# One of three norms moved from TensorE to VectorE, and the weight splits one step earlier

## What is computed

```python
def _gemma_mlp(x, gate_w, up_w, down_w):
    g = jnp.einsum('bsh,hi->bsi', x, gate_w)
    u = jnp.einsum('bsh,hi->bsi', x, up_w)
    return jnp.einsum('bsi,ih->bsh', jax.nn.gelu(g, approximate=True) * u, down_w)
rw = jax.nn.softmax(router_logits, axis=-1)
w, sel = jax.lax.top_k(rw, 2); w = w / w.sum(axis=-1, keepdims=True)
dense_w = zeros((B, E)).at[arange(B)[:, None], sel].add(w)
out = sum over e of dense_w[:, e, None, None] * _gemma_mlp(x, skill_gate[e], skill_up[e], skill_down[e])
return x + out + _gemma_mlp(x, shared_gate, shared_up, shared_down)
```

## Time and profile before

| | us |
|---|---|
| median of 3 runs (210.85 to 211.42) | 210.87 |
| the profiled execution: its time | 211.93 |
| the profiled execution: its span, first to last instruction | 210.1 |
| TensorE busy in the span | 205.2 |
| VectorE, ScalarE, GpSimd busy | 123.6, 133.8, 117.9 |

### The profile page before, as it was taken

The page is one execution under the profiler, slowest core; times in us unless marked ns, Lnnn a source line. Parts: engine busy times, 40 slices in busy tenths (PEclk is TensorE's granted clock), DMA queues, the critical chain, the costliest instruction groups (busy, mean ns, idle before and its releaser), DMA issues.

```text
span 210.1 us, 6672 instructions
## 1 busy us (share of the span) xinstructions
PE 205.2 (98%) x2695; PEld 165.0 (79%) x2695; DVE 123.6 (59%) x217; ACT 133.8 (64%) x217; POOL 117.9 (56%) x129
## 2 busy tenths in 40 slices
PE   7999999989999999999999999999999999999995
PEld 2444555445444478899999999999999999999995
DVE  2899657977999988554353444434435435344452
ACT  6283767677989997655656656556565565655650
POOL 3023644359548997665565655655656556565562
PEclk9999999999999999999999999999999999999999
DMA  6999600000000000000010010010010010010011
GB/s 196 391 433 434 296 2 0 0 3 0 2 0 5 0 0 3 0 3 5 3 53 3 0 53 3 3 53 0 3 55 3 3 53 0 3 53 4 3 50 53
DMA packets 2813, 11.70 MB, mean 56 GB/s; under 512 B 352, under 2 KB 608, under 8 KB 2400
## 3 DMA queue, kind: packets, MB, share of 16 engines
q1 hardware_dynamic: 2640, 11.01, 13.1%
q10 hardware_dynamic: 144, 0.26, 0.7%
HBM read 9.18 MB, written 2.10 MB: 54 GB/s over the span
## 4 chain that ended last, share of the span: by engine, by line
PE 93%; DVE 4%; issue 1%; ACT 0%; POOL 0%; POOLq 0%
PE o_ps L664 7%; PE g_ps L646 7%; PE u_ps L646 7%; PE o_ps L663 7%; PE u_ps L645 7%; PE g_ps L645 7%; PE u_ps L644 7%; PE g_ps L644 7%; PE o_ps L662 7%; PE u_ps L612 3%; PE g_ps L612 3%; PE g_ps L614 2%; PE o_ps L627 2%; PE o_ps L625 2%; PE o_ps L626 2%; PE g_ps L613 2%
## 5 line engine op out<-in xcount | busy, mean ns | idle before, releaser
L304 POOL TENSOR_TENSOR h<-h 128x512 f16<-128x512 f32 x92 | 109.2, 1194 | 79.2 <-ACT h L340 57.9
L457 DVE SCALAR_TENSOR_TENSOR h<-gel,sk_factor,u_ps 128x512 f32<-128x512 f32 x64 | 47.8, 747 | 68.0 <-PE u_ps L646 39.0
L335 ACT ACTIVATE gel<-g_ps,sk_gate 128x512 f32<-128x512 f32 x64 | 43.9, 687 | 49.8 <-PE g_ps L646 49.8
L340 ACT CAST h<-h 128x512 f16<-128x512 f32 x92 | 56.0, 609 | 3.5 <-DVE h L457 3.5
L645 PE MATMUL g_ps<-x,wsk 128*128 128x128 f16 x256 | 46.2, 219 | 0.0
L646 PE MATMUL g_ps<-x,wsk 128*128 128x128 f16 x256 | 46.2, 219 | 0.0
L645 PE MATMUL u_ps<-x,wsk 128*128 128x128 f16 x256 | 46.2, 219 | 0.0
L646 PE MATMUL u_ps<-x,wsk 128*128 128x128 f16 x256 | 46.2, 219 | 0.0
L644 PE MATMUL u_ps<-x,wsk 128*128 128x128 f16 x256 | 46.2, 219 | 0.0
L644 PE MATMUL g_ps<-x,wsk 128*128 128x128 f16 x256 | 46.2, 219 | 0.0
L663 PE MATMUL o_ps<-h,wsk 128*128 128x128 f16 x256 | 45.9, 219 | 0.0
(11 more groups left out here) (103 smaller groups left out, 310.1 us busy)
## 6 DMA issues: line engine op xcount, KB each, us to landing
wsk<-skills SPq DMA_DIRECT2D x3, 2048.0 KB, 16.1
outT<-xT SPq DMA_DIRECT2D x7, 256.0 KB, 2.0
xT<-xT SPq DMA_DIRECT2D x2, 768.0 KB, 6.3
wsh<-shared SPq DMA_DIRECT2D x3, 256.0 KB, 3.9
xT<-xT ACTq DMA_DIRECT2D x1, 256.0 KB, 3.5
xT<-xT SPq DMA_DIRECT2D x1, 256.0 KB, 4.6
outT<-xT SPq DMA_DIRECT2D x1, 192.0 KB, 2.6
outT<-xT SPq DMA_DIRECT2D x1, 64.0 KB, 1.5
```

The lines of the kernel that those rows point to most:

```text
L304: nc.gpsimd.tensor_tensor(hidden_lo(t), hidden_full(t), hidden_hi(t), ALU.subtract).then_inc(lo_ok, 1)
L335: nc.scalar.activation(gel[:, t % NG, :], g_ps[t % 2][:, :], ACT.Gelu_apprx_tanh, scale=scale).then_inc(gelu_ok, 1)
L340: nc.scalar.copy(hidden_hi(t), hidden_full(t)).then_inc(hi_ok, 1)
L457: nc.vector.scalar_tensor_tensor(out=h32[:, t % N32, :], in0=gel[:, t % NG, :], scalar=factor, in1=u_ps[t % 2][:, :], op0=ALU.mult, op1=AL ...
```

## The change

The norm of the experts' gate weights no longer comes from `gram`. VectorE takes the largest absolute value per partition over two experts at a time (128x1024) in steps 5, 6, 7 and 8 into a new tile `parts`, then the maximum of the four columns, its square, and `spread_norms` treats it as it does x. The norms of up and down keep their Gram matrices, taken in steps 9 to 12 (before 10 to 13) and 16 to 19 (before 15 to 18). The gate norm's mask is in step 8 (before 9) and its scales in step 10 (before 11); the mask and scales of down come a step later (20 and 22). The pieces of the experts' weights are split at steps 11, 13, ... 33 (before 12, 14, ... 34), the groups 4 to 7 of x at 12, 16, 20 and 24 (before 11, 15, 19, 23), and the experts' tables are made at step 24 (before 23).

```diff
+        parts = sb("parts", [P, E // 2], F32)
+        GRAMS = (K_UP, K_DOWN)
-        TOP_OF = {FIRST: 3 + XF, X_NEXT: 3 + XA, X_REST: 3 + G}
-        K_STEPS = [5, 10, 15]
-        MASK_AT = {3: X_NEXT, 9: K_GATE, 12: X_REST, 14: K_UP, 19: K_DOWN}
-        SPREAD_AT = {4: X_NEXT, 11: K_GATE, 14: X_REST, 16: K_UP, 21: K_DOWN}
+        TOP_OF = {FIRST: 3 + XF, X_NEXT: 3 + XA, X_REST: 4 + G, K_GATE: 4 + XA}
+        PART_AT = {5: (GATE, 0), 6: (GATE, 1), 7: (GATE, 2), 8: (GATE, 3)}
+        K_STEPS = {K_UP: 9, K_DOWN: 16}
+        MASK_AT = {3: X_NEXT, 8: K_GATE, 12: X_REST, 14: K_UP, 20: K_DOWN}
+        SPREAD_AT = {4: X_NEXT, 10: K_GATE, 14: X_REST, 16: K_UP, 22: K_DOWN}
-        SKILL_TABLES_AT = 23
-        X_AT = {3: 0, 5: 2, 8: 3, 11: 4, 15: 5, 19: 6, 23: 7}
+        SKILL_TABLES_AT = 24
+        X_AT = {3: 0, 5: 2, 8: 3, 12: 4, 16: 5, 20: 6, 24: 7}
-        PIECES = {12 + 2 * n: n for n in range(3 * E // EG)}
+        PIECES = {11 + 2 * n: n for n in range(3 * E // EG)}
...
+            def part_top(kind, n):
+                if n == 0:
+                    dve.wait_ge(sk_in[kind], 16)
+                nc.vector.tensor_reduce(parts[:, n:n + 1], wsk32[:, (kind * E + 2 * n) * I:(kind * E + 2 * n + 2) * I],
+                                        AX.X, ALU.max, apply_absolute_value=True).then_inc(part_ok, 1)
             def mask(n):
                 a, b = COLS[n]
-                if n not in K_OF:
+                if n in K_OF and n not in GRAMS:
+                    kind = K_OF.index(n)
+                    dve.wait_ge(part_ok, E // 2)
+                    tops(KC + kind, parts[:, :])
+                if n not in GRAMS:
                     dve.wait_ge(top_ok, TOP_OF[n])
                     nc.vector.tensor_tensor(top2[:, a:b], top[:, a:b], top[:, a:b], ALU.mult).then_inc(diag_ok, 1)
...
                     skill_low(PIECES[t - 1])
                 if t == 0:
                     scales(FIRST)
+                if t in PART_AT:
+                    part_top(*PART_AT[t])
                 if t in TOP_AT:
...
-                        if n == 0 and kind:
-                            pe.wait_ge(diag_ok, K_OF[kind - 1] + 1)
+                        if n == 0 and batch == K_DOWN:
+                            pe.wait_ge(diag_ok, K_UP + 1)
```

More of the change, by code:

```diff
@@ L141, in build @@
         top_ok = sem("top_ok")
+        part_ok = sem("part_ok")
         gram_ok = sem("gram_ok")
@@ L394, in mask @@
                 else:
-                    kind = K_OF.index(n)
-                    dve.wait_ge(gram_ok, kind + 1)
+                    dve.wait_ge(gram_ok, GRAMS.index(n) + 1)
                     nc.vector.scalar_tensor_tensor(out=diag[:, :], in0=n_ps[0][:, 0:P], scalar=NORM_FLOOR,
@@ L403, in scales @@
                 norm = n_ps[1][:, 0:b - a]
-                if n in K_OF:
+                if n in GRAMS:
                     norm = n_all[:, a:b]
                     nc.vector.tensor_reduce(norm, n_ps[1][:, 0:P], AX.X, ALU.max).then_inc(n_red, 1)
-                    dve.wait_ge(n_red, K_OF.index(n) + 1)
+                    dve.wait_ge(n_red, GRAMS.index(n) + 1)
                 nc.vector.tensor_scalar(e_bits[:, a:b], norm.bitcast(U32), 1, EXP_MASK,
@@ L698, in _ @@
                     down_first(1)
-                for kind in range(3):
-                    n = t - K_STEPS[kind]
+                for batch in GRAMS:
+                    kind = K_OF.index(batch)
+                    n = t - K_STEPS[batch]
                     if 0 <= n < 4:
@@ L703, in _ @@
                             pe.wait_ge(sk_in[kind], 16)
-                        if n == 0 and kind:
-                            pe.wait_ge(diag_ok, K_OF[kind - 1] + 1)
+                        if n == 0 and batch == K_DOWN:
+                            pe.wait_ge(diag_ok, K_UP + 1)
                         a = (kind * E + 2 * n) * I
                         for half in range(2):
-                            last = gram(n_ps[0][:, 0:P], wsk32[:, a + half * I:a + (half + 1) * I],
-                                        n == 0 and half == 0)
+                            last = gram(n_ps[0][:, 0:P], wsk32[:, a + half * I:a + (half + 1) * I], n == 0 and half == 0)
                         if n == 3:
```

## The result

The changed kernel takes 212.03 us (median of 8 runs, 211.67 to 212.82) against 211.12 for the kernel before (8 runs, 210.85 to 211.62): ratio 1.0045, 95% interval 1.0028 to 1.0062. It is slower by 0.9 us; no change was forecast, at 210.8, and the slower rival at 211.9 is what happened.

What follows compares the result with a forecast made beforehand. TensorE, busy 205.2 of 210.1 us, was taken as the bound. Four grams leave (1.86), but VectorE's maxima add 4.56 and waits take the gain: 0.1 less, 210.8 us from a 210.87 median; range 209.6 to 212.0.

Steps and rivals of the forecast that it cites:

- the slower rival: Step 14: GpSimd takes the port ahead of the scales, L412 is held 1.14 us; 211.9 us, chance 0.26.
- the maxima hold VectorE's queue for 1.14: Steps 5 to 8: each of four 128x1024 maxima taken as 1.14 us of VectorE, 4.56 against 4.20 idle.
- the down product of step 5: TensorE's product behind GpSimd's subtraction: starts at 25.47 instead of 25.03, after TensorE stands about 1.9 us.
- the square: VectorE's L393, due at 39.24, held by GpSimd's subtraction until 39.94, so the spread comes at 40.0 against 39.60.
- the second piece: Weight split on VectorE in step 14, held behind GpSimd's subtraction until 42.57, then about 1.1, ending at 43.65.
- three of the grams only filled a wait: Steps 5 to 7: of the four removed grams, 1.86 us, only the last, 0.47, would be gained even with shorter maxima.
- Steps 14 to 17: Up norm's mask at 44.33, spread at 44.48 after about 0.5 wait, gate(17) at 45.63 against 46.18: 0.08 ahead overall.
- VectorE falling behind at step 26: Late place where VectorE's dense steps move to; counted within the slower outcome's chance of 0.26, without its own size.
- What spoke against it: Step 14: at 42.63 L412 took only 0.15 beside the start of GpSimd's second subtraction in the kernel before.
- The other rival: The grams' time is kept (faster): about 1.0 less, 209.8 us; keeping all would be 208.0; chance 0.24.
- the down gram's wait: TensorE's 1.00 us before the first down gram at 43.26, saved by moving it a step, half taken back.
- the splits' new steps: Pieces one step earlier, VectorE's dense steps moved to 22 and 26: taken as nothing, 0.5 kept either way.

Runs made afterwards that it cites:

- e3: e4 without the four maxima: the tile of partition maxima is filled with a constant, so the gate norm is not computed; 209.52 us, ratio 0.9911.
- e1: The changed kernel, but in step 14 VectorE does the scales of x's last groups and the up norm's mask ahead of the second weight piece; 211.17 us, ratio 0.9987.
- e2: The changed kernel in its order, but the two scale instructions for x's last groups are written one column at a time; 211.42 us, ratio 1.0003.
- e5: The kernel before, with its Gram matrix for the gate norm, but the splits and experts' tables at the new steps; 215.92 us, ratio 1.0195.
- e4: The changed kernel with the norm by four maxima, but the splits and the experts' tables back at their old steps; 210.4 us, ratio 0.9949.
- e10: e1 with the maximum over x's last group in step 11 instead of 12; 210.89 us, ratio 0.9948 to the kernel before.
- e11: e4 with the maximum over x's last group in step 11 instead of 12; 210.58 us, ratio 0.9934 to the kernel before.
- e9: e4 with the gate maxima in steps 6 to 9, gate mask in 9, its scales in 11, and the maximum over x's last group in 11; 210.36 us, 0.9949.

## Why the prediction was wrong

Its route was right to within 0.14 us from 20.9 to 43.8 us. Forecast and measured: the maxima hold VectorE's queue for 1.14, 1.12 (21.54 to 22.66); `x_low` 23.34, 23.32; GpSimd 24.23, 24.21; the down product of step 5 25.47, 25.43; that of step 8 32.5, 32.56; the square 39.24, 39.38, held for 0.69; the spread 40.0, 40.12; the second piece ends at 43.65, 43.77. The reading that three of the grams only filled a wait is shown by e3.

The step that failed is in "Steps 14 to 17": "The scales of x follow (0.08 before that end, 0.18, 0.1 and the 0.19 of 42.63 to 42.82)". The last term, 0.19, is from the start of L412 to that of the mask, read where nothing held L412. Here it is 1.17 (43.95 to 45.12), because the same instruction, now L425, takes 1.14; the three terms ahead of it came as summed (0.08, 0.18, 0.08). So the mask ends at 45.41 instead of 44.33, the spread goes at 45.47 instead of 44.48, and gate(17) at 46.64 instead of 45.63: 0.08 ahead became 0.92 behind, which is the 0.9 us measured. e1 and e2 show that cause, each by another way round it, and e5 has the hold without the maxima.

The rival had this with its place and its price, at a chance of 0.26 (VectorE falling behind at step 26, counted in it, did not happen: TensorE does not wait there). What spoke against it was misread: in the kernel before, L412 at 42.63 came while L411 still waited for the first subtraction and ahead of the start of the second near 42.69 (41.54 + 1.15); here it came 0.04 after GpSimd's start. e4 has the first order again (42.38 ahead of 42.43, 0.15), e5 the second (43.63 behind 43.59, 1.14). My own numbers put the two at 43.80 and 43.85, in the order that loses, and a duration from a case in which VectorE was first was no evidence for one in which it was second. With that order the rival should have been the forecast. The range, drawn up to that rival's price, ended 0.03 below the measured time. The kernel before took 211.12 beside this result and 210.87 beside the forecast, so that 0.03 says little; what was wrong is the difference of the two kernels, 0.9 us slower where 0.1 faster was summed.

The other rival's reasoning holds in part: the 1.00 of the down gram's wait was there to win, but only once nothing held the mask (e4).

Nothing was taken for the splits' new steps as such, and e10 against e11 shows that this was near enough: their stretches differ by 0.39, and 0.5 was kept for it.

## What to carry to other kernels

Where two engines share a port that one instruction locks whole, the price of a small instruction is set by who starts first, so work out both starts and order them before choosing a duration; a tiny instruction that stands right behind the one that sets off the other engine is the one to move. Work taken from the busiest engine is worth what its next wait leaves: look for slack of a tenth of a microsecond at places where the timeline shows no wait at all. When a schedule's steps are moved, redo who stands next to whom in each queue, and not only whether the sum of the work fits.

## What was not expected of the hardware

In e5 TensorE stood from 42.46 to 45.24 us, and the granted clock was still 1.00 while it stood. It fell only after the work had begun again: 0.67 in 45.5 to 46.0 and 0.50 (1.2 of 2.4 GHz) in 46.0 to 49.0, where 512-wide matmuls follow each other at 0.42 instead of 0.22 us, and it was back at 1.00 from 49.3. This execution took 216.35 us with a mean clock of 0.992. Two more of the six of e5 have that mean clock and took 216.41 and 216.75; the other three have 1.00 and took 214.76 to 215.49. So the fall goes with about 1.5 us more (between the medians of the two kinds, 216.41 and 214.88); that it came at the same wait in the two that have no trace is not shown. In the changed kernel the clock is 1.00 through the window with its 1.4 us wait.

Two instructions of a single column behave differently beside GpSimd: with a subtraction running, the 128x1 tensor_scalars of e2 take 0.20 for two and 0.14 for one, and the 128x1 tensor_tensor of e9, with two inputs in SBUF, is held for 1.07.
